# Row sums once a quarter behind a product with V, their pair sums accumulated on VectorE, and four conversions moved between VectorE, ScalarE and GpSimd

## The chip, the cores and the metric

One core of a Trainium2 chip runs the whole layer. The time is what one execution takes on the device, in microseconds (us). PE is TensorE (PEld its weight loads), DVE is VectorE, ACT is ScalarE, POOL is GpSimd, SP is SyncE, which here only issues DMAs.

## The reference

A transformer layer with causal attention (ALiBi bias) and a mixture of experts side by side on the same normed input. Batch 4, 1024 tokens, width 512, 16 heads of 32, 8 experts of inner size 352, two per token.

```
xn = layernorm(x)
q, k, v = (xn @ W.T + b) per head            # 4 x 16 heads x 1024 x 32
scores = q @ k.T / sqrt(32), causal, - slope_h * |i - j|
out = (softmax(scores) @ v) @ Wo.T + bo
combine = top 2 of softmax(xn @ gate_w.T), normalised
moe = sum_e combine_e * ((silu(g_e) * u_e) @ w2_e.T),   g_e, u_e = xn @ w1_e.T
return x + out + moe
```

Softmax is computed without its division: P = exp(scores - bound), O = P V, and the row sums R = P 1; O is divided by R at the end. The bias of v can be added before the product (each row of P/R sums to one) or after the division.

## The kernel before

Numbers that enter TensorE in the projections, the scores and the experts are split into two float16 halves, high and low, and multiplied in three passes. P and V stay float32.

Attention goes through 16 groups `G` (4 batches x 4 groups of four heads), each in 40 units `u` of one head: a unit's scores are 256 keys by 256 queries (three or four matmuls, L1266 to L1271), then one exp on ScalarE (L1864) from one of two PSUM halves `C` into `PT[t % 3]`. Four units, one for each head, make a tile `t`: tile `(q, i)` holds key pair `i` of query quarter `q`, with `i` from 0 to `q`. So a group has ten tiles; four of them (`i == q`) lie on the diagonal, and there only three of the four 128 x 128 blocks are computed (the exp is 384 wide, not 512). A quarter's product with V and its row sums gather in one of two PSUM banks, `O` and `M`, in columns 0 to 255 and 256 to 511.

For each tile GpSimd adds the two key blocks (`add`, L1984, 1024 elements a partition, 512 on the diagonal) into one of three buffers `PS`. TensorE multiplies the tile by V (`pv`, L1284) and, later, the sum by a block of ones (`rsum`, L1294; on the diagonal L1296 and L1297). Four heads go to four column strips of 32. The profile shows each of these float32 matmuls as two MATMUL instructions, so a group of 8 instructions is one row sum of four heads.

After a quarter's last row sum ScalarE copies the bank out (`osb`, L1895), a DMA folds the sums, VectorE inverts them (`rcp`, L1680), a DMA and a matmul (`bc`, L1306) spread them, VectorE scales (`a32`, L1684), and GpSimd splits the result into halves (`aT`: a cast, L1994, and a subtraction, L1995) for the output projection (L1318, evicted at L1691).

Beside this run, for the next groups: the projections of q and k (L1205; evicted by ScalarE at L1842 as `qk32`, rounded to the high half by VectorE at L1644 as `qkh`, low half on GpSimd at L1973 as `qkl`), V (L1222; evicted by VectorE at L1657 as `vsb`, bias added there), the row maxima that bound the scores (`pre` on TensorE, L1238 and L1243; `mx` on VectorE, L1671, and a small `join`, L1676), the layernorm of the next batch (its low half `xnl` on VectorE, L1556), the splitting of the expert weights (L1906 on ScalarE, L1725 on VectorE) and the routing (among it L1742). All but the tile sums and the two banks `C`, `O`/`M` share four PSUM banks `PB`: a bank is borrowed for a product and given back when its reader (VectorE, now and then ScalarE) is done.

The order is written out by a planner, `plan()`: it walks through the units, adds a unit's score and exp, fires events that were put at this unit (`at(u, f)`), and fills in projections by a credit of TensorE time. Every engine issues its own steps in this one order and never passes a step that waits. After the last unit come the output projection of the last batch and 71 slots of expert work, the stage from about 1155 us on.

## Time and profile before

| | |
|---|---|
| median of 3 runs | 1599.04 us (1596.22 to 1602.14) |
| profiled execution, its own time | 1600.13 us |
| its span, first to last instruction | 1598.3 us |
| mean granted TensorE clock | 0.966 of full |
| busy in the span: PE, DVE, POOL, ACT | 1465.1, 936.9, 848.4, 703.9 us |

1.8 us of the execution lie outside the span. Busy time is the union of an engine's instructions. The ends of matmuls are modelled and they overlap, so the distance from the start of one group of matmuls to the start of the next says more than a duration does. "Idle before" of a group of instructions is idle time of its engine just ahead of them, with what ended it; "issue" there means that no wait in the profile accounts for it.

### The profile page before, as it was taken

What the parts mean: (1) busy time and instruction counts of PE and PEld (TensorE: products, weight loads), DVE (VectorE), ACT (ScalarE), POOL (GpSimd) and SP (SyncE); (2) the same over time, 40 slices, a digit from 0 to 9 for tenths busy, and PEclk for the clock granted to TensorE, in tenths of its full rate; (3) what the DMA queues carried; (4) which work ended last, traced back from release to release, by engine and by line L of the source; (5) the groups of instructions that cost most, each with busy time, mean ns of one, the idle gap of its engine ahead of it and who ended that gap; (6) DMA issues with size and microseconds to landing.
All of it is one profiled execution on the core that took longest, in us unless ns stands there. A gap on an engine that the chain in (4) does not pass through costs nothing.

```text
span 1598.3 us, 35194 instructions
## 1 busy us (share of the span) xinstructions
PE 1465.1 (92%) x13499; PEld 862.9 (54%) x13499; DVE 936.9 (59%) x1765; ACT 703.9 (44%) x1179; POOL 848.4 (53%) x732
## 2 busy tenths in 40 slices
PE   4689989998998999999999899897789999999995
PEld 2356555654655565555565456553356565655663
DVE  7667877766687666668768976560143333333331
ACT  5245565545556555556664444465022222222221
POOL 5134555444454454545564446575117777668774
PEclk9899998999998999999999999998899999999998
DMA  7244433443524426343233310233867888889983
GB/s 252 57 130 135 140 94 108 119 132 105 161 81 116 136 85 209 92 126 102 89 107 112 100 41 16 68 126 101 303 161 131 133 129 137 125 120 148 147 138 44
DMA packets 189309, 193.92 MB, mean 121 GB/s; under 512 B 104900, under 2 KB 138948, under 8 KB 189021
## 3 DMA queue, kind: packets, MB, share of 16 engines
q1 hardware_dynamic: 160636, 152.27, 35.6%
q0 software_dynamic: 26128, 37.24, 14.0%
q8 instruction: 115, 1.88, 0.5%
q10 hardware_dynamic: 2384, 2.16, 0.4%
q14 instruction: 46, 0.37, 0.1%
HBM read 93.14 MB, written 53.74 MB: 92 GB/s over the span
## 4 chain that ended last, share of the span: by engine, by line
PE 67%; DVE 11%; DMA 8%; ACT 4%; issue 4%; POOL 3%; SPq 2%; ACTq 0%; another core or an unknown queue 0%; DVEq 0%; POOLq 0%
PE S L1356 13%; PE T L1205 4%; PE S L1205 4%; PE M L1284 4%; PE O L1387 4%; PE M L1387 4%; PE S L1238 3%; DVE arena L1671 3%; PE T L1238 3%; PE S L1266 3%; DMA arena<-arena 3%; PE O L1284 3%; DMA out<-arena 2%; PE T L1222 2%; PE T L1318 2%
## 5 line engine op out<-in xcount | busy, mean ns | idle before, releaser
L1864 ACT ACTIVATE arena<-S,psl 128x512 f32<-128x512 f32 (+1 forms) x640 | 401.8, 642 | 359.2 <-PE S L1268 194.4
L1984 POOL TENSOR_TENSOR arena<-arena 128x1024 f32<-128x1024 f32 (+1 forms) x160 | 312.3, 1954 | 215.9 <-ACT arena L1864 215.4
L2038 POOL DMA_INDIRECT out<-arena x142 | 222.1, 1564 | 110.2 <-issue 46.7
L1356 PE MATMUL S<-arena 128*128 x1704 | 267.4, 314 | 6.1 <-issue 4.9
L1671 DVE TENSOR_REDUCE arena<-S 128x1 f32<-128x512 f32 (+3 forms) x311 | 202.8, 656 | 103.5 <-PE S L1243 53.2
L1671 DVE TENSOR_REDUCE arena<-T 128x1 f32<-128x512 f32 (+3 forms) x297 | 193.7, 656 | 87.1 <-PE T L1243 49.1
L1356 PEld LDWEIGHTS S<-arena 128*128 128x128 f16 x1704 | 166.8, 98 | 103.7 <-issue 7.4
L1266 PE MATMUL S<-arena 106*128 106x256 f16 x640 | 179.3, 280 | 22.4 <-ACT arena L1864 21.2
L1973 POOL TENSOR_TENSOR arena<-arena 128x512 f16<-128x512 f32 x64 | 78.9, 1233 | 153.9 <-DVE arena L1644 153.7
L1783 DVE COPY arena<-T 128x512 f16<-128x512 f16 x71 | 30.2, 425 | 219.8 <-PE T L1371 181.9
L1238 PE MATMUL T<-arena 105*128 105x512 f16 (+3 forms) x382 | 113.1, 333 | 25.0 <-DMA arena<-in_up 10.1
L1917 ACT ACTIVATE arena<-S,sc 128x352 f32<-128x352 f32 x71 | 39.3, 553 | 206.4 <-PE S L1356 191.6
L1238 PE MATMUL S<-arena 105*128 105x512 f16 (+3 forms) x386 | 119.2, 341 | 9.7 <-DVE arena L1671 5.1
L1205 PE MATMUL T<-arena 128*128 128x512 f16 x420 | 108.3, 386 | 1.7 <-DVE arena L1671 0.7
L1266 PEld LDWEIGHTS S<-arena 106*128 106x128 f16 x640 | 63.6, 99 | 80.4 <-ACT arena L1864 38.7
L1994 POOL CAST arena<-arena 128x256 f16<-128x256 f32 x64 | 27.2, 425 | 150.2 <-DVE arena L1684 150.0
L1268 PE MATMUL S<-arena 106*128 106x256 f16 x384 | 106.7, 279 | 0.0
L1284 PE MATMUL M<-arena 128*32 128x256 f32 (+1 forms) x1536 | 99.3, 376 | 0.0
L2025 POOL DMA_INDIRECT arena<-xn_d,tl x71 | 72.6, 1023 | 43.9 <-DMA arena<-arena 22.3
L1205 PE MATMUL S<-arena 128*128 128x512 f16 x348 | 92.0, 388 | 1.9 <-DVE arena L1671 1.9
L1725 DVE SCALAR_TENSOR_TENSOR arena<-arena,sc 128x704 f16<-128x704 f32 (+2 forms) x56 | 70.0, 1250 | 34.5 <-ACT arena L1906 34.2
L1925 ACT ACTIVATE arena<-arena 128x352 f16<-128x352 f32 x71 | 35.2, 496 | 109.4 <-DVE arena L1769 101.7
(218 smaller groups left out, 2517.3 us busy)
## 6 DMA issues: line engine op xcount, KB each, us to landing
arena<-arena SPq DMA_DIRECT2D x192, 128.0 KB, 2.8
arena<-in_w1T SPq DMA_DIRECT2D x64, 352.0 KB, 3.6
arena<-in_x SPq DMA_DIRECT2D x64, 256.0 KB, 4.4
w_d<-arena SPq DMA_DIRECT2D x32, 352.0 KB, 2.8
arena<-w_d SPq DMA_DIRECT2D x16, 704.0 KB, 6.7
arena<-in_w2T SPq DMA_DIRECT2D x32, 256.0 KB, 3.0
out<-arena SPq DMA_DIRECT2D x32, 256.0 KB, 3.2
xn_d<-arena SPq DMA_DIRECT2D x24, 256.0 KB, 2.6
```

The source lines that it names most:

```text
L1205: tp = pe.matmul(z[:, :], wqkv[:, w_, c, f:f + P], xnT[:, a, c, half * 512:half * 512 + 512], start=(third == 0 and c == 0), stop=(third = ...
L1238: tp = pe.matmul(z[:, n * w:(n + 1) * w], stk[G % 2][0:KROWS - 1, h, 0, j * P:(j + 1) * P], stk[G % 2][0:KROWS - 1, h, 1, k0:k1], start=(n ...
L1266: pe.matmul(z[:, 0:2 * P], K[0], stk[G % 2][0:KROWS, h, 0, q0:q2], start=True, stop=False)
L1268: tp = pe.matmul(z[:, 2 * P:4 * P], K[1], stk[G % 2][0:KROWS, h, 0, q0:q2], start=False, stop=True)
L1284: tp = pe.matmul(YB[o.bank["pv", G, q]][D * x:D * x + D, f:f + n], V[(G + 1) % 3][:, 2 * i + k, x * D:(x + 1) * D], PT[t % 3][:, x, c:c + ...
L1356: tp = pe.matmul(y[:, i * 512:i * 512 + I], xT[:, s % XDEEP, 4 * a + c, :], weights[:, bass.ds(reg[s] + (w_ * NX * W1N + c * 2 * I + i * I ...
L1387: tp = pe.matmul(z[:, :], aTm[0:n, v, 2 * c + a, :], weights[0:n, bass.ds(r2 + (2 * NX * W1N + w_ * NX * W2N + c * E), E)], start=(k == 0) ...
L1671: dve.tensor_reduce(d[:, heads[0]:heads[-1] + 1], z, AX, ALU.max).then_inc(sems["mx"], 1)
L1864: act.activation(PT[t % 3][:, h, 0:n], CB[o.bank["score", u]][:, 0:n], ACT.Exp, scale=psl[:, hh:hh + 1]).then_inc(sems["exp"], 1)
L1973: pool.tensor_tensor(st[:, 2 * qk + 1, lo:hi], t32_at(*key), st[:, 2 * qk, lo:hi], ALU.subtract).then_inc(sems["qkl"], 1)
L1984: pool.tensor_tensor(PS[t % 3][:, :, f:f + n], PT[t % 3][:, :, f:f + n], PT[t % 3][:, :, c:c + n], ALU.add).then_inc(sems["add"], 1)
L2038: pool.indirect_dma_start(out=halves, out_offset=bass.IndirectOffsetOnAxis(row[:, part, s:s + 1].bitcast(U32), 0), in_=yo[:, s % YDEEP, c0 ...
```

## The change

Row sums. For a quarter's first tile GpSimd adds the two key blocks into an accumulator `AC[q % 2]` (for quarter 0 a copy and an add of 512). For a later tile it adds them into a buffer, `PSF` (whole tiles) or `PSD` (diagonal), one of each, and a new VectorE step `acc` adds this buffer to the accumulator; on the diagonal GpSimd itself adds the first block, so its one add becomes two of 512. TensorE multiplies the accumulator by ones once a quarter, in the step that comes behind the next tile's product with V. The exp no longer waits for a row sum.

Conversions. `qkh` and `vsb` go from VectorE to ScalarE; `vsb` becomes a plain scaled copy, and the bias of v is added in a new ScalarE step `aTh` (two ACTIVATEs of 128 x 256), which also makes the high half that GpSimd's cast made. The low half `xnl` goes from VectorE to GpSimd for the later batches. One load (`bvb`) at the start goes. Some distances in the plan are a unit or two longer.

```diff
             at(u + 1, lambda: add("add", t))
+            if i:
+                at(u + 4, lambda: add("acc", t))
             at(4 * t + 5, lambda: products(t))
-            at(4 * t + (10 if i < q else 9), lambda: sums(t))
+            if t == QUADS - 1:
+                at(4 * t + 9, lambda: sums(t))
...
         add("pv", t)
+        if i == 0 and t:
+            sums(t - 1)
...
-        if i == q:
-            at(now[0] + 1, lambda: emptied(G, q))
+        at(now[0] + 1, lambda: emptied(G, q))
...
-                add("aT", G, q)
-                ready["aT", G, q] = now[0] + 2
+                at(now[0] + 1, lambda: add("aTh", G, q))
+                at(now[0] + 2, lambda: add("aT", G, q))
+                ready["aT", G, q] = now[0] + 4
...
                 on.wait_ge(*at("add", t))
+                if i:
+                    on.wait_ge(*at("acc", t))
                 for x in range(4):
-                    R = YB[o.bank["pv", G, q]][D * x:D * x + D, 2 * P:4 * P]
-                    if i < q:
-                        tp = pe.matmul(R, ones, PS[t % 3][:, x, :], start=False, stop=False)
-                    else:
-                        pe.matmul(R[:, 0:P], ones, PT[t % 3][:, x, 0:P], start=False, stop=False)
-                        tp = pe.matmul(R[:, P:2 * P], ones, PS[t % 3][:, x, P:2 * P], start=False, stop=True)
+                    tp = pe.matmul(YB[o.bank["pv", G, q]][D * x:D * x + D, 2 * P:4 * P], ones, AC[q % 2][:, x, :],
+                                   start=False, stop=True)
...
+            elif kind == "acc":
+                t, = key
+                G, q, i = quad(t)
+                on.wait_ge(*at("add", t))
+                f, z = (0, PSF) if i < q else (P, PSD)
+                if i > 1:
+                    on.wait_ge(*at("acc", t - 1))
+                dve.tensor_tensor(AC[q % 2][:, :, f:], AC[q % 2][:, :, f:], z, ALU.add).then_inc(sems["acc"], 1)
...
+                act.activation(st[:, 2 * qk, lo:hi], t32_at(*key), ACT.Copy).then_inc(sems["qkh"], 1)
...
+                act.activation(V[(G + 1) % 3][:, 4 * half:4 * half + 4, :].rearrange("p a n -> p (a n)"),
+                               PB[o.bank["v", b, g, half]][:, :], ACT.Copy, scale=col(CV)).then_inc(sems["vsb"], 1)
...
+                a_ = osb[:, q % 2, 0:2 * P]
+                act.activation(aT[:, 0, g, 2 * q * P:2 * (q + 1) * P], a_, ACT.Identity, bias=bvs[:, g:g + 1])
+                act.activation(a_, a_, ACT.Identity, bias=bvs[:, g:g + 1]).then_inc(sems["aTh"], 1)
...
+                elif i < q:
+                    if t > 10:
+                        on.wait_ge(*at("acc", t - 1 if i == 2 else t - 3 if q == 3 else t - 6))
+                    elif i == 2 or q == 3:
+                        on.wait_ge(*at("acc", t - 1 if i == 2 else t - 3))
+                    pool.tensor_tensor(PSF, y[:, :, 0:2 * P], y[:, :, 2 * P:4 * P], ALU.add).then_inc(sems["add"], 1)
+                else:
+                    if G or q > 1:
+                        on.wait_ge(*at("acc", t - (3, 3, 4)[q - 1]))
+                    pool.tensor_tensor(PSD, y[:, :, P:2 * P], y[:, :, 2 * P:3 * P], ALU.add)
+                    if i > 1:
+                        on.wait_ge(*at("acc", t - 1))
+                    else:
+                        on.wait_ge(*at("add", t - 1))
+                    pool.tensor_tensor(z[:, :, 0:P], z[:, :, 0:P], y[:, :, 0:P], ALU.add).then_inc(sems["add"], 1)
```

How this moves instructions is shown at three places. First TensorE, around unit 466, where a whole tile's row sum stood by itself between two units. Before (L1266 and L1268 are scores, L1294 the row sum, L1238 a piece of the maxima, L1222 the projection of V, L1306 `bc`, L1253 a transposition of maxima):

```order
L1266 MATMUL S<-arena 128x256 [waits s_exp]
L1268 MATMUL S<-arena 128x256
L1294 MATMUL O<-arena,cF 32x256 [waits s_add]
L1294 MATMUL O<-arena,cF 32x256 x3
L1238 MATMUL T<-arena 128x512 [waits s_mx]
L1222 MATMUL S<-arena 128x128 x12
L1266 MATMUL S<-arena 128x256 [waits s_exp]
L1268 MATMUL S<-arena 128x256
L1306 MATMUL T<-arena 128x256 [waits s_unfold1,s_mx]
L1253 MATMUL S<-cF,arena 4x128 [waits s_mx]
L1253 MATMUL S<-cF,arena 4x128
```

The same units now (lines are those of the new file: L1271 and L1273 scores, L1243 the maxima, L1227 V, L1309 `bc`, L1258 the transposition):

```order
L1271 MATMUL S<-arena 128x256 [waits s_exp]
L1273 MATMUL S<-arena 128x256
L1243 MATMUL T<-arena 128x512 [waits s_mx]
L1227 MATMUL S<-arena 128x128 x12
L1271 MATMUL S<-arena 128x256 [waits s_exp]
L1273 MATMUL S<-arena 128x256
L1309 MATMUL T<-arena 128x256 [waits s_unfold1,s_mx]
L1258 MATMUL S<-cF,arena 4x128 [waits s_mx]
L1258 MATMUL S<-cF,arena 4x128
```

The row sum is gone from there, and with it a change between the two shapes of matmul. The quarter's one row sum (L1299) stands three units later, at the end of the quarter, behind the next quarter's first product (L1289):

```order
L1271 MATMUL S<-arena 128x256 [waits s_exp]
L1273 MATMUL S<-arena 128x256
L1289 MATMUL M<-arena 32x256 [waits s_osb]
L1289 MATMUL M<-arena 32x256 x7
L1299 MATMUL O<-arena,cF 32x256 [waits s_acc,s_add]
L1299 MATMUL O<-arena,cF 32x256 x3
L1243 MATMUL S<-arena 128x512 [waits s_mcp]
L1227 MATMUL S<-arena 128x128 x12
```

It follows the product at once and waits for VectorE's `acc` as well as for GpSimd's `add`. Second VectorE, from one `a32` to the next around the middle of attention. Before (L1684 `a32`, L1671 maxima, L1644 `qkh`, L1725 a weight's low half, L1680 `rcp`):

```order
L1684 TENSOR_TENSOR arena<-arena,T 128x256 [waits s_bc]
L1671 TENSOR_REDUCE arena<-S 128x1 [waits s_pre]
L1671 TENSOR_REDUCE arena<-T 128x1 [waits s_pre]
L1680 RECIPROCAL arena<-arena 128x8 [waits s_fold1]
L1671 TENSOR_REDUCE arena<-S 128x1 [waits s_pre] x2
L1644 CAST arena<-arena 128x512 [waits s_qk32]
L1725 SCALAR_TENSOR_TENSOR arena<-arena,sc 128x704 [waits s_wsh]
L1671 TENSOR_REDUCE arena<-S 128x1 [waits s_pre]
L1671 TENSOR_REDUCE arena<-T 128x1 [waits s_pre,s_mtr]
L1671 TENSOR_REDUCE arena<-S 128x1 [waits s_pre] x2
L1657 SCALAR_TENSOR_TENSOR arena<-T,sc,arena 128x512 [waits s_pv,s_v]
L1684 TENSOR_TENSOR arena<-arena,T 128x256 [waits s_bc]
```

Now, up to the same `a32` (L1664; L1643 maxima, L1660 `rcp`, L1656 `acc`, L1705 a weight's low half):

```order
L1643 TENSOR_REDUCE arena<-S 128x1 [waits s_pre]
L1643 TENSOR_REDUCE arena<-T 128x1 [waits s_pre]
L1643 TENSOR_REDUCE arena<-S 128x1 [waits s_pre]
L1660 RECIPROCAL arena<-arena 128x8 [waits s_fold1]
L1643 TENSOR_REDUCE arena<-S 128x1 [waits s_pre]
L1656 TENSOR_TENSOR arena<-arena 128x1024 [waits s_add]
L1643 TENSOR_REDUCE arena<-S 128x1 [waits s_pre]
L1705 SCALAR_TENSOR_TENSOR arena<-arena,sc 128x704 [waits s_wsh]
L1643 TENSOR_REDUCE arena<-T 128x1 [waits s_pre,s_mtr]
L1643 TENSOR_REDUCE arena<-S 128x1 [waits s_pre] x2
L1656 TENSOR_TENSOR arena<-arena 128x4x128 [waits s_acc,s_add]
L1664 TENSOR_TENSOR arena<-arena,T 128x256 [waits s_bc]
```

`qkh` and `vsb` (L1657) have left the queue, and two `acc`, which wait for GpSimd's `add`, stand ahead of maxima that free banks for TensorE. Third ScalarE, in the second group. Before (L1864 exp, L1871 a row of maxima, L1842 `qk32`):

```order
L1871 ACTIVATE arena<-S 4x256 [waits s_mrow2,s_mtr]
L1842 ACTIVATE arena<-T,bq,cq 128x512 [waits s_qk,s_qkl]
L1864 ACTIVATE arena<-S,psl 128x384 [waits s_score,s_add,s_pv]
L1864 ACTIVATE arena<-S,psl 128x384 [waits s_score] x3
L1864 ACTIVATE arena<-S,psl 128x512 [waits s_score,s_add,s_pv]
```

Now (L1875 exp, L1882 a row of maxima, L1822 `qk32`, L1855 and L1856 `aTh`, L1832 `qkh`):

```order
L1882 ACTIVATE arena<-S 4x256 [waits s_mrow2,s_mtr]
L1822 ACTIVATE arena<-T,bq,cq 128x512 [waits s_qk,s_qkl]
L1875 ACTIVATE arena<-S,psl 128x384 [waits s_score,s_add,s_pv]
L1875 ACTIVATE arena<-S,psl 128x384 [waits s_score]
L1855 ACTIVATE arena<-arena,bvs 128x256 [waits s_a32]
L1856 ACTIVATE arena<-arena,bvs 128x256
L1832 ACTIVATE arena<-arena 128x512 [waits s_stack12,s_stack11,s_stack13,s_stack10,s_qk32]
L1875 ACTIVATE arena<-S,psl 128x384 [waits s_score] x2
```

Between two exps stand three instructions more, and two of the waits are for VectorE and for DMAs (`stack`).

## Rows read from the trace of the kernel before

**Rows 1.** Busy us (instructions) by stretch: PE, PEld, DVE, ACT, POOL; then clock, DMA share, GB/s.
```profile
130.00:1080.00 950.00, 899.67 (x9472) 531.19 (x9465) 678.51 (x1218) 512.82 (x854) 487.95 (x441) 0.97 0.38 109
200.00:800.00 600.00, 567.12 (x5977) 330.92 (x5973) 417.72 (x691) 338.87 (x561) 297.69 (x289) 0.96 0.40 117
800.00:960.00 160.00, 152.88 (x1552) 90.19 (x1552) 130.66 (x310) 79.59 (x134) 79.91 (x63) 0.99 0.32 90
```

**Rows 2.** What PE waited for, 130 to 1080 us: in total, times, longest.
```profile
PE S L1266 <- ACT arena L1864: 10.8, 12, 2.3
PE T L1238 <- DVE arena L1671: 4.1, 7, 1.2
...
PE S L1253 <- DVE arena L1671: 0.4, 1, 0.4
```

**Rows 3.** PE in order of time: start, length, instructions merged.
```profile
646.97 0.64 PE L1294 MATMUL O<-arena,cF 128*32 128x256 f32 x8
647.54 0.39 PE L1238 MATMUL S<-arena 105*128 105x512 f16 x1
...
657.68 0.45 PE L1296 MATMUL O<-arena,cF 128*32 128x128 f32 x8
657.92 0.42 PE L1297 MATMUL O<-arena,cF 128*32 128x128 f32 x8
658.14 1.07 PE L1284 MATMUL M<-arena 128*32 128x256 f32 x16
659.14 0.39 PE L1238 MATMUL S<-arena 105*128 105x512 f16 x1
```

**Rows 4.** Row sums of whole tiles, by line: count, busy us, mean ns, idle before.
```profile
L1294 PE MATMUL M<-arena,cF 128*32 128x256 f32 x512 | 42.2, 402 | 2.5 <-POOL arena L1984 2.5
L1294 PE MATMUL O<-arena,cF 128*32 128x256 f32 x256 | 20.9, 399 | 0.0
```

**Rows 5.** VectorE's groups that leave, or are nearest to what comes.
```profile
L1644 DVE CAST arena<-arena 128x512 f16<-128x512 f32 x64 | 40.1, 627 | 10.9 <-ACT arena L1842 5.9 <-DMA arena<-arena 4.8
L1657 DVE SCALAR_TENSOR_TENSOR arena<-S,sc,arena 128x512 f32<-128x512 f32 x17 | 12.7, 746 | 1.4 <-PE S L1222 1.2
L1556 DVE TENSOR_TENSOR arena<-arena 128x512 f16<-128x512 f32 x24 | 17.9, 746 | 2.9 <-ACT arena L1798 2.1
L1742 DVE TENSOR_TENSOR arena<-cF,posf 128x1024 f32<-128x1024 f32 x8 | 12.7, 1589 | 0.0
L1676 DVE TENSOR_TENSOR arena<-arena 128x8 f32<-128x8 f32 x32 | 18.6, 581 | 1.1
```

**Rows 6.** Shortest, median and longest ns, first and last start: two VectorE lines, GpSimd's `add`.
```profile
L1742 DVE TENSOR_TENSOR arena<-cF,posf x8: 1215/1549/2114, 940.7 to 1019.5; 128x1024 f32<-128x1024 f32 x8
L1676 DVE TENSOR_TENSOR arena<-arena x32: 166/168/2346, 78.9 to 1082.0; 128x8 f32<-128x8 f32 x32
L1984 POOL TENSOR_TENSOR arena<-arena x160: 1257/2354/3021, 87.3 to 1120.2; 128x1024 f32<-128x1024 f32 x96, 128x512 f32<-128x512 f32 x64
```

**Rows 7.** GpSimd and VectorE in order of time around one small add.
```profile
469.63 4.67 POOL L1984 TENSOR_TENSOR arena<-arena 128x1024 f32<-128x1024 f32 x2
469.67 2.35 DVE L1676 TENSOR_TENSOR arena<-arena 128x8 f32<-128x8 f32 x1
```

**Rows 8.** ScalarE's groups, for the price of what is moved there.
```profile
L1864 ACT ACTIVATE arena<-S,psl 128x512 f32<-128x512 f32 x384 | 258.4, 686 | 205.0 <-PE S L1268 194.4 <-DVE arena L1680 3.0 <-remote 2.9
L1864 ACT ACTIVATE arena<-S,psl 128x384 f32<-128x384 f32 x256 | 146.0, 577 | 154.2 <-PE S L1271 150.7 <-PE O L1284 1.4 <-ACT arena L1895 0.7
L1798 ACT ACTIVATE arena<-arena 128x512 f16<-128x512 f32 x32 | 19.6, 627 | 38.1 <-DVE arena L1550 38.1
L1933 ACT ACTIVATE arena<-O,tl 128x512 f32<-128x512 f32 x36 | 24.2, 672 | 6.7 <-PE O L1387 6.7
```

**Rows 9.** GpSimd's groups.
```profile
L1994 POOL CAST arena<-arena 128x256 f16<-128x256 f32 x64 | 27.2, 425 | 150.2 <-DVE arena L1684 150.0
L1964 POOL TENSOR_TENSOR arena<-arena 128x512 f16<-128x512 f32 x8 | 9.5, 1210 | 3.3 <-ACT arena L1798 3.3
```

109 lines of the change are left out of this document (51 added, 58 removed).

## The prediction, written before the changed kernel was run

> **What bounds the kernel.** I read four views, in this order. The busy times by stretch [rows 1]: while attention runs with its fill (130 to 1080 us) TensorE is busy 899.7 of 950 us, VectorE 678.5, ScalarE 512.8, GpSimd 488.0. Then what TensorE waited for in that stretch [rows 2]: 10.8 us for exps, and 23.0 us in fourteen rows (4.1 to 0.4 us each, the first and the last are shown) for VectorE to give back a bank, with a few single waits beside them. A wait for GpSimd's `add` hardly exists (2.5 us over the whole run [rows 4]). So TensorE sets the pace from 130 to 1080 us, and time taken from it comes off the end as long as nobody else falls behind. The reader should see there that VectorE is second, with 71% on average and 82% between 800 and 960 us (130.7 of 160 [rows 1]), where the routing runs. The expert stage after about 1155 us is touched nowhere by the change; I price it at nothing.
>
> **TensorE: what leaves.** A matmul's length says little, since they overlap; I go by starts. The row sum of a whole tile is 8 instructions; there are 768 of them, 96 groups, busy 42.2 + 20.9 = 63.1 us, 0.66 us a group [rows 4]. All are removed. A diagonal row sum is 16 instructions of half the width and stands directly ahead of the next product: from its start at 657.68 to the product's at 658.14 are 0.46 us [rows 3]. Four a group of heads, 64 in all: 29.4 us.
>
> **TensorE: what comes.** 64 row sums of 8 instructions, each behind a product of the same shape (256 columns, 32-wide strips). A product of 16 such instructions takes 1.00 us from its start to the next start (658.14 to 659.14), a lone row sum of 8 takes 0.57 (646.97 to 647.54) [rows 3]. Both end with the same change to another shape of matmul, so 8 more instructions in one run cost the difference, 0.43 us. Below it lies what 8 half-wide ones take (657.68 to 657.92, 0.24 [rows 3]), above it a lone group's 0.66. 64 x 0.43 = 27.5 us (15 to 42). TensorE's balance: 63.1 + 29.4 - 27.5 = 65.0 us less (50 to 77).
>
> **VectorE.** It loses 64 roundings of q and k (40.1 us), 32 copies of V (12.7 us for 17, 23.9 for all by the same 0.746), and 24 low halves (17.9) [rows 5]: 81.9 us. It gains 96 `acc`: six a group of heads, half with 1024 elements, half with 512. Nothing in the trace is this instruction. The nearest with 1024 float32 elements and two operands in SBUF is L1742: 1.215 us at best, 1.589 in the mean; an add of 8 elements, L1676, takes 0.166 at best [rows 5, 6], and half-way between them lies 0.69 for 512. These, 1.215 and 0.69, are the lower ends. The upper ends come from what such adds suffer here: the one of 8 elements takes 0.168 us in the median and 2.346 at worst [rows 6], and that worst one began 0.04 us after the first of two GpSimd adds and ended when that one did (4.67 us for two [rows 7]). So a whole GpSimd add, 2.34 us, may come on top: 3.56 and 3.03 us. The mean of the small add is 0.581, which is 0.41 above its median [rows 5, 6]; I take 1.59 and 0.69 + 0.41 = 1.10. 48 x 1.59 + 48 x 1.10 = 129 us (91 to 316). Net VectorE has 47 us more to do (9 to 234).
>
> The Trainium skill bears on this: "SBUF — State Buffer", section "Who interferes with whom", says that a VectorE instruction with two SBUF inputs contends with a GpSimd instruction that reads SBUF, and that whichever starts first keeps the shared ports for its whole length. The trace agrees with that in the 2.35 us of the small add. By that rule the delay also goes the other way, and `acc` holds up GpSimd's adds; this is the third rival below, whose numbers are from rows 6 and 7.
>
> Does it fit? A group of heads takes 65 us now (160 tiles, ten a group, whose adds start from 87.3 to 1120.2 [rows 6], so 6.5 us a tile) and gains 65.0 / 16 = 4.1 us; VectorE gets 129 / 16 = 8.1 and loses 4.0 (without `xnl`). From 200 to 800 us (9.2 groups): 417.7 + 38 - 18 = 438 of 562 us, 78% instead of 70%. From 800 to 960 us (2.5 groups): 130.7 + 10.1 = 141 of 150 us, 94% instead of 82%. In that last stretch I give back half of the 10 us gained: 5 us. Elsewhere the 23 us that TensorE waits for VectorE's banks grow: idle room on VectorE shrinks from 29 to some 20%, and I let the waits grow by half: 12 us (0 to 40). `acc` waits for GpSimd's `add`, and the maxima that free the banks are queued behind it. It is issued three units after the `add`, 4.6 us, against the add's 2.34 us (2.5 for the diagonal's two, by 1.257 each [rows 6]), so mostly it finds its operand ready. The row sum on TensorE waits for `acc`, issued two units (3.1 us) ahead; with 1.1 to 1.6 us for it a late VectorE shows here first, and scores are queued behind: 2 us.
>
> **ScalarE.** 64 `qkh`, SBUF to SBUF with 512 elements, at 0.627 (L1798): 40.1 us. 32 `vsb` at 0.672 (a scaled PSUM copy, L1933): 21.5. 128 halves of `aTh` with 256 elements: the exp shows 0.686 for 512 and 0.577 for 384, so 0.468 for 256: 59.9 [rows 8]. Together 121 us, no bounds needed beyond a tenth either way. In 130 to 1080 us that makes about 627 of 911 us, 69% instead of 54%. An exp may start later by up to two of these (1.3 us) and TensorE has two score halves, so two units of 1.5 us cover it, except where an exp was already late (10.8 us of waits [rows 2]); I add 6 us (0 to 20). `aTh` waits for VectorE's `a32` with exps queued behind it, so a late VectorE reaches the scores here too. In the 6 us are also the two waits of 4.8 us in all for the stack DMAs [rows 5], which now stop exps instead of maxima.
>
> **GpSimd.** 48 adds of 512 more at 1.257 [rows 6] (60 us), 16 copies at about twice the cast's 0.425 (14), 24 `xnl` at 1.21 (29), less 64 casts (27) [rows 9]: 76 us more, about 558 of 911 us in the stretch, 61%. Its new waits are for `acc` of an earlier tile, since there is one buffer, with `qkl` and `aT` queued behind; by the order that `acc` is issued a unit before. Its own queue does not get long; what it costs others is in the terms above.
>
> **The ends.** At the start the first four roundings take ScalarE 0.627 each as they take VectorE in the mean, but stand in a queue with its other conversions: 0.8 us, an estimate of one more of them ahead. In the tail the last quarter's chain has two ScalarE instructions of 0.47 in place of a cast of 0.42: 0.5 us.
>
> **The sum.** 65.0 gained; 5 + 12 + 2 + 6 + 1.3 = 26 given back; 39 us less. Against the profiled execution's own 1600.1 us (span 1598.3 and 1.8 around it): 1561 us. The median of the runs, 1599.0, is 1.1 lower, too close to matter; I say 1560.
>
> **Rivals.**
> First, it all converts: `acc` and the ScalarE steps fall into idle time. For it: no engine but TensorE is over 82% in any stretch. Against: queues are strict, and VectorE and TensorE already wait for each other in both directions. 1600 - 65 + 1.3 gives 1536 us.
> Second, VectorE becomes the bound in good part: it is the second engine, it gets 47 us net, and the banks hang on it. Price: the waits for banks grow by 36 us instead of 12, and all 10 us between 800 and 960 us are lost. 1561 + 24 + 5 gives about 1588 us.
> Third, slower than before: the accumulations and GpSimd's adds block each other. `acc` for tile t comes about when GpSimd begins the add of tile t + 1, if VectorE lags by a unit. Each of 96 then waits up to 2.34 us [rows 6, 7] with maxima behind it, a bank is kept, and TensorE stops. It decides from 65 / 96 = 0.68 us of TensorE standing still per `acc`. At 1.0 us each it is 96 us against 65, and 1600 + 31 gives 1631 us. Against it: the mean wait of the small adds is 0.41 us, well under 0.68, and four banks give slack.
> Fourth, no change: TensorE is not the bound although it looks busy. PEld is busy only 531 of 950 us [rows 1], and a chain through exps and banks could set the pace, with the row sums in its gaps. Against it: TensorE's named waits are some 40 us, so there are no gaps for 92 us of row sums. 1598 us. The Trainium skill takes that side: "Perfetto Trace Analysis", section "Identifying the Most-Contended Engine", calls matmul occupancy a bad measure of the distance to the roofline and asks for the weight loads' share, here 56%. By the waits of this trace the queue is full all the same.
>
> **Chances.** My forecast (1548 to 1578) 0.50; all converts 0.18; VectorE bound 0.20; no change 0.05; slower 0.07. The second and third of these cover 1530 to 1548 and 1578 to 1592. The range from 1536 to 1592 leaves out the last two cases (0.12) and a little below and above, 0.2 in all, and it takes in the bounds of the row sum's price and of the waits. A measurement here can tell 0.5%, 8 us, from no change: faster 0.87, within 0.5% 0.05, slower 0.08.
>
> **What would show it.** Right: TensorE's busy time falls by about 65 us and all of the loss of span lies ahead of 1120 us; row sums are 512 instructions of some 27 us; `acc` has a mean near 1.3 us with a longest one over 3; VectorE is 90% busy or more in the routing stretch; TensorE's waits for VectorE's banks and for exps come to 50 us or so. If `acc` lies at its lower ends and the bank waits stay at 23 us, the first rival holds. If TensorE shows long waits for `acc` at the row sum, or if it falls to the lower clock in attention for long, my sum is wrong: neither is in it but for 2 us.

## The result

The changed kernel takes 1601.0 us in the median of 20 runs (1595.9 to 1607.1), against 1594.4 us for the kernel before on the same chip (20 runs); the ratio is 1.0041 with an interval of [1.0022, 1.0059]. So it is no faster, and slower by a trifle, below the 0.5% at which the prediction drew its line. The prediction was 1560 us, with 1536 to 1592 as its range. It was wrong.

### The profile page after: what moved, and what is told of

Read it like the earlier page. It is cut to its first block, busy times and chain, and to the rows that moved or that the text cites. A ratio compares the mean times of both kernels' runs of the same rounds, so it can differ in the third digit from the quotient of the medians.

```text
span 1595.9 us, 32893 instructions
## 1 busy us (share of the span) xinstructions
PE 1419.4 (89%) x12219; PEld 838.9 (53%) x12219; DVE 947.9 (59%) x1742; ACT 799.1 (50%) x1403; POOL 948.4 (59%) x756
## 4 chain that ended last, share of the span: by engine, by line
PE 55%; DVE 13%; POOL 11%; DMA 7%; issue 6%; ACT 4%; SPq 4%; ACTq 0%; POOLq 0%; DVEq 0%
PE S L1359 15%; PE O L1390 4%; PE M L1390 4%; DVE arena L1643 4%; PE T L1210 3%; DVE arena L1656 3%; DMA arena<-arena 3%; PE M L1289 3%; PE S L1210 3%; PE S L1243 2%; SPq L1059 2%; PE T L1243 2%; PE S L1271 2%; PE O L1289 2%; POOL arena L2006 2%
## 5 line engine op out<-in xcount | busy, mean ns | idle before, releaser
L1875 ACT ACTIVATE arena<-S,psl 128x512 f32<-128x512 f32 (+1 forms) x640 | 399.5, 641 | 256.0 <-PE S L1273 152.2
L1643 DVE TENSOR_REDUCE arena<-S 128x1 f32<-128x512 f32 (+3 forms) x311 | 202.0, 655 | 113.5 <-PE S L1248 82.4
L1643 DVE TENSOR_REDUCE arena<-T 128x1 f32<-128x512 f32 (+3 forms) x297 | 193.0, 654 | 95.5 <-PE T L1248 65.3
L1271 PE MATMUL S<-arena 106*128 106x256 f16 x640 | 182.0, 285 | 40.7 <-ACT arena L1875 39.2
L1999 POOL TENSOR_TENSOR arena<-arena 128x512 f32<-128x512 f32 (+1 forms) x64 | 135.7, 2121 | 81.5 <-ACT arena L1875 81.4
L1984 POOL TENSOR_TENSOR arena<-arena 128x512 f16<-128x512 f32 x64 | 79.9, 1250 | 165.2 <-ACT arena L1832 165.0
L2006 POOL TENSOR_TENSOR arena<-arena 128x1024 f32<-128x1024 f32 x48 | 114.8, 2392 | 75.4 <-ACT arena L1875 46.9
L1243 PE MATMUL S<-arena 105*128 105x512 f16 (+3 forms) x386 | 120.3, 345 | 21.8 <-DVE arena L1643 12.7
L1243 PE MATMUL T<-arena 105*128 105x512 f16 (+3 forms) x382 | 115.8, 342 | 26.4 <-DMA arena<-in_up 10.4
L1656 DVE TENSOR_TENSOR arena<-arena 128x512 f32<-128x512 f32 (+1 forms) x96 | 110.3, 1148 | 36.0 <-POOL arena L2015 19.4
L1271 PEld LDWEIGHTS S<-arena 106*128 106x128 f16 x640 | 64.4, 101 | 103.1 <-ACT arena L1875 61.4
L1273 PE MATMUL S<-arena 106*128 106x256 f16 x384 | 107.3, 280 | 0.0
L2051 POOL DMA_INDIRECT arena<-xn_d,tl x71 | 73.1, 1030 | 46.3 <-DMA arena<-arena 25.8
L1289 PE MATMUL M<-arena 128*32 128x256 f32 (+1 forms) x1536 | 100.3, 380 | 0.0
L2010 POOL TENSOR_TENSOR arena<-arena 128x512 f32<-128x512 f32 x48 | 67.9, 1415 | 41.6 <-ACT arena L1875 41.5
```

The costliest lines, as they stand in the source:

```text
L1243: tp = pe.matmul(z[:, n * w:(n + 1) * w], stk[G % 2][0:KROWS - 1, h, 0, j * P:(j + 1) * P], stk[G % 2][0:KROWS - 1, h, 1, k0:k1], start=(n ...
L1271: pe.matmul(z[:, 0:2 * P], K[0], stk[G % 2][0:KROWS, h, 0, q0:q2], start=True, stop=False)
L1289: tp = pe.matmul(YB[o.bank["pv", G, q]][D * x:D * x + D, f:f + n], V[(G + 1) % 3][:, 2 * i + k, x * D:(x + 1) * D], PT[t % 3][:, x, c:c + ...
L1643: dve.tensor_reduce(d[:, heads[0]:heads[-1] + 1], z, AX, ALU.max).then_inc(sems["mx"], 1)
L1656: dve.tensor_tensor(AC[q % 2][:, :, f:], AC[q % 2][:, :, f:], z, ALU.add).then_inc(sems["acc"], 1)
L1875: act.activation(PT[t % 3][:, h, 0:n], CB[o.bank["score", u]][:, 0:n], ACT.Exp, scale=psl[:, hh:hh + 1]).then_inc(sems["exp"], 1)
```

## The profile after

Two of the stretches of [rows 1] again, of the changed kernel, with the same columns:

```profile
130.00:1080.00 950.00, 855.09 (x8255) 506.95 (x8254) 684.24 (x1194) 591.33 (x1046) 581.49 (x464) 0.95 0.37 108
800.00:960.00 160.00, 146.23 (x1374) 86.82 (x1375) 133.87 (x311) 92.67 (x166) 95.23 (x65) 0.98 0.33 92
```

TensorE is busy 44.6 us less in the same 950 us, and the work gets no further in them: that is idle time. Over the whole execution its busy time fell from 1465.1 to 1419.4 us, by 45.7 and not by 65, and the span from 1598.3 to 1595.9 us. The difference between 65 and 45.7 is the clock, as far as an estimate can tell. In the two profiled executions it stood at 0.966 in the mean before and stands at 0.952 now; with full speed (2.4 GHz) or half (1.2 GHz) as its two levels that is (1 - 0.966) x 2 x 1598 = 109 us at half speed before, and 153 us after. In 44 more such microseconds work that needs 22 at full speed is done, so 22 us are added to busy time: 65 - 22 = 43, and 45.7 is seen. (The kernel below with only the conversions moved has the same matmuls as the kernel before and checks this: 109 us at half speed before and 78 there should make 15 us less of busy time, and 1465.1 - 1449.0 = 16.1 us is seen.) Of the 45.7 us that left busy time only 2.4 left the span; the other 43.3 us became idle time.

What TensorE waited for from 130 to 1080 us in the changed kernel, columns as in [rows 2]:

```profile
PE S L1271 <- ACT arena L1875: 29.0, 22, 4.3
PE S L1243 <- DVE arena L1643: 10.9, 9, 2.9
PE M L1299 <- DVE arena L1656: 7.9, 4, 3.9
PE T L1243 <- DVE arena L1643: 7.1, 5, 3.5
PE S L1258 <- DVE arena L1643: 5.1, 1, 5.1
PE S L1243 <- DVE arena L1664: 4.6, 5, 1.9
...
PE O L1299 <- DVE arena L1656: 1.1, 1, 1.1
```

Scores waiting for exps (L1271 for L1875) are 29.0 us where they were 10.8 [rows 2]; row sums waiting for `acc` (L1299 for L1656) are 9.0 us, which is new. All rows in which TensorE waits for VectorE add up to 44.4 us against the 23.0 of [rows 2]: 29.4 for maxima (L1643; 20.0 before), 6.0 for `a32` (L1664; 3.0 before) and these 9.0 for `acc`.

One part of why exps are late stands in ScalarE's own waits in the same stretch:

```profile
ACT arena L1906 <- POOL arena L2021: 14.1, 5, 4.3
ACT arena L1855 <- DVE arena L1664: 8.0, 6, 3.7
ACT arena L1832 <- DMA arena<-arena: 7.9, 4, 5.2
```

L1906 is `osb`, the copy of a quarter's output to SBUF. It may not overwrite its buffer until GpSimd's `aT` (L2021) has read it, and exps are queued behind it. The other two are `aTh` behind `a32`, and `qkh` behind the stack's DMAs (7.9 us; the maxima waited 4.8 for them before [rows 5]).

The groups of instructions that the change made, columns as in [rows 4]:

```profile
L1656 DVE TENSOR_TENSOR arena<-arena 128x1024 f32<-128x1024 f32 x48 | 68.8, 1434 | 16.6 <-POOL arena L2006 16.1
L1656 DVE TENSOR_TENSOR arena<-arena 128x512 f32<-128x512 f32 x48 | 41.4, 863 | 19.4 <-POOL arena L2015 19.4
L1299 PE MATMUL M<-arena,cF 128*32 128x256 f32 x256 | 21.5, 409 | 7.9 <-DVE arena L1656 7.9
L1299 PE MATMUL O<-arena,cF 128*32 128x256 f32 x256 | 21.2, 403 | 1.1 <-DVE arena L1656 1.1
L1832 ACT ACTIVATE arena<-arena 128x512 f16<-128x512 f32 x64 | 40.0, 626 | 8.0 <-DMA arena<-arena 7.9
L1855 ACT ACTIVATE arena<-arena,bvs 128x256 f16<-128x256 f32 x64 | 32.0, 501 | 29.5 <-DVE arena L1664 29.4
L2006 POOL TENSOR_TENSOR arena<-arena 128x1024 f32<-128x1024 f32 x48 | 114.8, 2392 | 75.4 <-ACT arena L1875 46.9 <-DVE arena L1656 28.2
L2015 POOL TENSOR_TENSOR arena<-arena 128x512 f32<-128x512 f32 x48 | 67.0, 1397 | 7.0 <-DVE arena L1656 7.0
```

`acc` took 110.2 us (68.8 + 41.4), under the 129 predicted. Ahead of it VectorE stood idle 35.5 us for GpSimd's adds, and GpSimd stood idle 35.2 us for `acc` (the last two rows). Each engine waits for the other.

One such meeting, all engines in order of time (start, length, instruction; idle time before it and what ended it in brackets):

```profile
1036.98 0.42 PE L1271 MATMUL S<-arena 106*128 106x256 f16 x1
1037.19 0.42 PE L1273 MATMUL S<-arena 106*128 106x256 f16 x1
...
1038.44 0.27 PE L1271 MATMUL S<-arena 106*128 106x256 f16 x1
1038.56 0.27 PE L1273 MATMUL S<-arena 106*128 106x256 f16 x1
...
1039.20 1.07 PE L1289 MATMUL O<-arena 128*32 128x256 f32 x16
1039.42 1.28 POOL L2015 TENSOR_TENSOR arena<-arena 128x512 f32<-128x512 f32 x1
1040.65 2.35 POOL L1999 TENSOR_TENSOR arena<-arena 128x1024 f32<-128x1024 f32 x1
1040.74 2.81 DVE L1656 TENSOR_TENSOR arena<-arena 128x512 f32<-128x512 f32 x1 [2.82 <-POOL arena L2015]
1043.47 0.41 DVE L1664 TENSOR_TENSOR arena<-arena,T 128x256 f32<-128x256 f32 x1
1043.69 0.64 PE L1299 MATMUL M<-arena,cF 128*32 128x256 f32 x8 [3.42 <-DVE arena L1656]
...
1043.91 0.51 ACT L1855 ACTIVATE arena<-arena,bvs 128x256 f16<-128x256 f32 x1 [3.70 <-DVE arena L1664]
```

GpSimd ends a diagonal's second add at about 1040.7 and begins its next add, 2.35 us long, at once. VectorE, which had waited 2.82 us for the first, starts `acc` 0.09 us behind the second and is through 0.55 us after it ended: 2.81 us for 512 elements, of which the shortest took 0.64. TensorE stood 3.42 us at the row sum, with every score queued behind, and ScalarE 3.70 us at `aTh`. The first two pairs show the clock: from one matmul's start to the next are 0.21 us at 1037 and 0.12 at 1038.5, the same instruction at half and at full clock (granted 0.52 of full from 1036.5 to 1038.0 and 1.00 from 1038.4 to 1039.2).

The second meeting has the wait of `osb` in it, which the kernel before never showed, again in order of time:

```profile
496.21 0.19 POOL L1966 TENSOR_TENSOR nw<-nw 128x4 f32<-128x4 f32 x1
...
499.91 0.22 POOL L1970 TENSOR_SCALAR nw<-nw 128x4 f32<-128x4 f32 x1
500.21 1.15 POOL L1984 TENSOR_TENSOR arena<-arena 128x512 f16<-128x512 f32 x1
...
501.33 2.33 POOL L1999 TENSOR_TENSOR arena<-arena 128x1024 f32<-128x1024 f32 x1
501.34 2.61 DVE L1553 TENSOR_SCALAR arena<-arena,mv,nw 128x512 f32<-128x512 f32 x1
503.63 0.84 POOL L2021 TENSOR_TENSOR arena<-arena 128x256 f16<-128x256 f32 x1
...
504.47 0.53 DVE L1553 TENSOR_SCALAR arena<-arena,mv,nw 128x512 f32<-128x512 f32 x1
504.50 0.60 ACT L1906 ACTIVATE arena<-M 128x512 f32<-128x512 f32 x1 [4.27 <-POOL arena L2021]
505.00 0.68 ACT L1875 ACTIVATE arena<-S,psl 128x512 f32<-128x512 f32 x1
505.73 0.40 PE L1271 MATMUL S<-arena 106*128 106x256 f16 x1 [4.35 <-ACT arena L1875]
```

Ahead of `aT` GpSimd's queue has thirteen small instructions of the next batch's layernorm (L1966 to L1970, from 496.21 to 500.13), then `qkl` (L1984) and one pair sum (L1999); ScalarE waits 4.27 us at `osb`, and TensorE 4.35 us for the exp behind it. Three of the five waits of `osb`, 12.7 of the 14.1 us, stand behind this same sequence, once in each batch that has a next one. The kernel before has the same small instructions and never waits there, since its cast and subtraction stand ahead of the next pair sum; the changed plan puts `aT` two units later, behind `aTh`. With only the conversions moved the three waits are 2.2 us each; with row sums accumulated the diagonal's second add stands ahead of the small instructions, and they are 4.2. Beside GpSimd's add even VectorE's scaling of x (L1553) takes 2.61 us; the next one, alone, 0.53.

## The experiments

All ratios are against the kernel before, from the same chip, with their 95% intervals; microseconds between two kernels are the difference of their ratios times 1595. A difference of two is uncertain by some 5 to 8 us. The first kernel is the one before with one edit, as are two later ones; the others start from the changed kernel. Where a kernel leaves out part of the row sums, its result is wrong and only its time is used; that is said with it. The stretch from 130 to 1080 us is a fixed piece of time: in a kernel that is faster it holds some of what comes behind attention, so waits and idle time are compared between kernels over the whole execution, in the table behind the experiments.

### Row sums behind the next product, nothing else

```
-            at(4 * t + (10 if i < q else 9), lambda: sums(t))
+            if t == QUADS - 1:
+                at(4 * t + 9, lambda: sums(t))
...
         add("pv", t)
+        if t:
+            sums(t - 1)
```

> The kernel before with each tile's row sum put directly behind the next tile's product with V; the work is the same, only 96 changes of matmul shape go. If TensorE is the bound: 96 x (0.66 - 0.43) = 22 us less, about 1573 us. If it is not: within 8 us of before.

Measured: 1588.6 us, 0.9955 [0.9936, 0.9974], 7 us less. A place behind a product is worth that, with every row sum kept, and not the 22 us of the first theory: TensorE's busy time fell from 1465.1 to 1449.3 us, and its idle time grew by 8.5 us.

### The conversions moved, the row sums as before

The changed kernel without `acc`, with row sums, pair sums and their buffers as before (the later places of `aTh` and `aT` and the other distances of the new plan stay):

```
-            if i:
-                at(u + 4, lambda: add("acc", t))
-            if t == QUADS - 1:
-                at(4 * t + 9, lambda: sums(t))
+            at(4 * t + (10 if i < q else 9), lambda: sums(t))
```

> The changed kernel with the row sums as before (no accumulation on VectorE, three pair-sum buffers, a row sum for every tile), so the moved conversions alone. Theory 1 (the accumulation ate the gain): no slower than before, 1590 to 1600 us, or a little faster, since VectorE has 82 us less to do. Theory 2 (ScalarE and GpSimd became late with the moved work): 20 to 50 us slower than before.

Measured: 1575.8 us, 0.9888 [0.9861, 0.9914], 18 us less. Its stretch of 130 to 1080 us:

```profile
130.00:1080.00 950.00, 904.95 (x9658) 534.01 (x9656) 595.72 (x1121) 613.84 (x1081) 506.35 (x419) 0.98 0.38 111
```

TensorE is busier than before (904.95 against 899.67 us) at a better clock, with VectorE 83 us lighter and ScalarE 101 us heavier. Over the whole execution its waits for VectorE fall from 27.0 to 14.8 us and its scores' waits for exps stay at 21.2 us, although `osb` waits 7.8 us for `aT` here already:

```profile
ACT arena L1897 <- POOL arena L1993: 7.8, 6, 2.2
```

The part of the change that the prediction booked mostly as a cost is its gain.

### Without accumulations

```
-            if i:
-                at(u + 4, lambda: add("acc", t))
...
-                if i:
-                    on.wait_ge(*at("acc", t))
```

> The changed kernel without the VectorE accumulation: pair sums are still formed on GpSimd, in the same number of instructions, but those of later whole tiles are dropped, and a row sum waits for GpSimd alone. Theory 1: the 65 us appear, 1535 to 1550 us. Theory 2: only the accumulation's own small waits go, 1585 to 1600 us.

Measured: 1554.4 us, 0.9763 [0.9733, 0.9794]. GpSimd's waits for `acc` are gone too, and on the diagonal it writes its sum straight into the accumulator; the row sums lack what `acc` would have added. `acc` and its waits cost the difference to the changed kernel, 0.0278 or 44 us.

### Accumulations of two elements a head, all waits kept

```
-                dve.tensor_tensor(AC[q % 2][:, :, f:], AC[q % 2][:, :, f:], z, ALU.add)
+                dve.tensor_tensor(z[:, :, 0:2], z[:, :, 0:2], PSF[:, :, 0:2], ALU.add)
```

> The changed kernel with the accumulation on VectorE cut to 2 of 256 (or 128) elements a head: every instruction and every wait of it stays, its length goes (most of the row sum is left out; on the diagonal GpSimd writes its sum instead of VectorE adding it). Theory A (the waits between GpSimd, VectorE and TensorE cost the time): it stays near the changed kernel, 1590 to 1600 us. Theory B (the time on VectorE and at the shared ports costs it): it falls to the kernel without accumulation, 1554 to 1565 us.

Measured: 1567.2 us, 0.9826 [0.9794, 0.9859]. Here too GpSimd writes the diagonal's sum straight into the accumulator. The waits, with instructions of some 0.3 us each (28.0 us in all), cost 10 us over the kernel without `acc`.

### Accumulations that read one input

A maximum over the same elements into four numbers stands in place of each addition:

```
+                z = PSF if i < q else AC[q % 2][:, :, P:]
+                dve.tensor_reduce(scr[:, :], z, AX, ALU.max).then_inc(sems["acc"], 1)
```

> As the kernel with the tiny accumulation, but each accumulation is a maximum over the same 1024 or 512 elements of one buffer: about as long on VectorE as the real one, with one operand in SBUF instead of two (its result is thrown away). If the length on VectorE costs the time (B1): 1585 to 1600 us. If the contention of two-operand adds with GpSimd costs it (B2): near 1555 to 1570 us, and GpSimd's adds come down from 2.39 us toward their 2.34.

Measured: 1586.2 us, 0.9938 [0.9913, 0.9962]. Its substitutes, by shortest, median and longest in nanoseconds, and below them the real `acc` of the changed kernel:

```profile
L1657 DVE TENSOR_REDUCE scr<-arena x96: 645/944/1221, 106.8 to 1115.6; 128x4 f32<-128x512 f32 x48, 128x4 f32<-128x1024 f32 x48
```

```profile
L1656 DVE TENSOR_TENSOR arena<-arena x96: 642/1210/2836, 105.0 to 1126.4; 128x512 f32<-128x512 f32 x48, 128x1024 f32<-128x1024 f32 x48
```

As in the two kernels before this one, row sums are incomplete. With one input none is ever stretched (1.221 at most); with two, the same bulk takes up to 2.836 us. The length alone costs 18 us over the tiny ones, and the step to the real `acc` another 16 us, though the 96 instructions got only 110.2 - 90.6 = 19.6 us longer. That step is called the second input below, but it also brings an output of full width in place of four numbers; no run has the two apart.

### The accumulation on GpSimd instead

```
-                    pool.tensor_tensor(PSF, y[:, :, 0:2 * P], y[:, :, 2 * P:4 * P], ALU.add)
+                    then(pool.tensor_tensor(z, z, y[:, :, 0:2 * P], ALU.add))
+                    pool.tensor_tensor(z, z, y[:, :, 2 * P:4 * P], ALU.add)
```

> The changed kernel with the accumulation on GpSimd instead of VectorE: two adds of 1024 for a later whole tile, three of 512 on the diagonal. GpSimd gets 48 x 2.39 = 115 us more, VectorE 110 us less. If VectorE's queue was what took the gain and GpSimd has room (581 + 115 of 950 us): 1560 to 1575 us. If GpSimd's adds now hold up the exps through the three tile buffers: 1600 us or more.

Measured: 1628.5 us, 1.0202 [1.0169, 1.0234]. The stretch:

```profile
130.00:1080.00 950.00, 834.76 (x8101) 500.22 (x8103) 619.14 (x1088) 578.84 (x1022) 695.25 (x535) 0.95 0.36 103
```

GpSimd is busy 73% of it, no engine is full, and it is the slowest kernel of all: another 26 us over the changed one. Its trace shows one large new wait of TensorE in the same stretch:

```profile
PE T L1163 <- POOL arena L1963: 22.6, 8, 8.7
PE S L1163 <- POOL arena L1963: 14.9, 4, 8.0
```

L1163 are the transpositions of the next batch's x, and L1963 is `xnl`, which the change moved to GpSimd and which now stands behind two or three adds a tile. These waits are 37.5 us; in the changed kernel they are 4.0.

### Conversions moved and row sums behind the products

> The conversions moved, row sums for every tile as before but each directly behind the next product with V. By the two alone (0.9888 and 0.9955 of before) 0.984, about 1570 us; if the freed VectorE lets TensorE use what the 96 saved changes of shape give (22 us), 1560 us.

The first two edits together. Measured: 1567.6 us, 0.9841 [0.9803, 0.9878]. With all the work in it, this is the fastest version that computes the reference: 25 us under the kernel before, at a clock of 0.976. What the two gained apart, 18 and 7 us, adds up.

### 48 row sums fewer in the kernel before

This and the next ask what the prediction took for granted: does time taken from TensorE come off the end?

```
-            at(4 * t + (10 if i < q else 9), lambda: sums(t))
+            if i in (0, q):
+                at(4 * t + (10 if i < q else 9), lambda: sums(t))
```

> The kernel before, with the row sums of the 48 whole tiles that are neither a quarter's first nor its diagonal left out (384 of the 768 matmul instructions of that line; the sums come out too small). TensorE has 48 x 0.66 = 31.5 us less work and no other engine has an instruction more or less. What the prediction took for granted, that TensorE sets the pace of attention: 1594 - 31 = 1563 us, ratio 0.980. The rival, that the chain of scores, maxima and exps sets it and the row sums stand in its gaps: 1585 to 1594 us, ratio 0.994 to 1.000, with the idle time of TensorE between 130 and 1080 us up by about what its busy time lost.

(With all 96 left out the results are no longer finite, and there is no time for it.) Measured: 1577.2 us, 0.9869 [0.9839, 0.9900]: 21 us of 31.5, between both expectations. The stretch, and the score's wait in it:

```profile
130.00:1080.00 950.00, 888.54 (x9214) 532.88 (x9210) 679.38 (x1226) 518.76 (x869) 495.01 (x448) 0.96 0.38 110
```

```profile
PE S L1267 <- ACT arena L1865: 21.2, 20, 2.3
```

No other engine's work was touched. It is tempting to set the 21.2 us against the 10.8 of [rows 2], and the idle time of 61.5 us against 50.3; but attention ends 18 us earlier here, so this stretch holds 18 us of later work more, and the kernel before has ten of its microseconds of waits for exps behind 1080 us. Over the whole executions the scores' waits for exps are

```profile
PE S L1266 <- ACT arena L1864: 21.2, 21, 2.5
PE S L1267 <- ACT arena L1865: 25.8, 25, 2.3
```

and TensorE's idle time grows by 3.2 us only, from 133.2 to 136.4. The larger part of the missing third is in the clock: 0.958 against 0.966 in the two profiles makes 133 us at half speed against 109, so 12 us of the 31.5 come back as slower work. Over all runs the mean granted clock is 0.962 against 0.967, which makes 8 us of it.

### The same 48 fewer, with the conversions moved

> The kernel with the conversions moved alone, with the same 48 row sums left out; again only TensorE loses work, 31.5 us of it. The conversions alone took 1576 us (0.989) at a granted clock of 0.975. If TensorE sets the pace there: 1576 - 31 = 1545 us, ratio 0.969. If freed time on TensorE turns into idle time and half clock: 1565 to 1576 us, ratio 0.982 to 0.989, with a granted clock under 0.975. The kernel changed without accumulations left out 54 of 65 us of row sums and stood at 0.976, so I expect something near 0.978.

Measured: 1554.3 us, 0.9731 [0.9708, 0.9755], 25 us of 31.5 over the conversions alone. That more of it converts with VectorE lighter (25 us against 21) is within what these differences are uncertain by, so it is not shown.

### Low halves of x alone, and all conversions but them

```
-            elif kind == "xnl" and key[0]:
...
-                dve.tensor_tensor(XH[k][:, E:2 * E], x_place(b, half, i), XH[k][:, 0:E],
-                                  ALU.subtract).then_inc(sems["xnl"], 1)
...
-            elif kind == "xnl" and not key[0]:
+            elif kind == "xnl":
```

> The kernel before with one conversion moved: the 24 low halves of x that VectorE made (17.9 us) are made by GpSimd. In the kernel before TensorE stood idle 7.7 us in the 24 transposes around them, with the conversions moved not at all. Theory: this is most of the gain of the conversions, 0.5 us a transpose and the scores behind it: 1582 to 1586 us, ratio 0.992 to 0.995. Rival: the gain comes from VectorE being freed of q, k and V (64 us of the 82), and this alone gives 1590 to 1594 us, ratio 0.998 to 1.000.

Measured: 1592.2 us, 0.9982 [0.9964, 1.0000], 3 us. The second kernel is the conversions without this edit.

> The conversions moved alone, but with the 24 low halves of x kept on VectorE as in the kernel before. Theory that the low halves made the gain: 1584 to 1590 us, ratio 0.994 to 0.997. Rival, that freeing VectorE of q, k and V made it: 1576 to 1581 us, ratio 0.989 to 0.992.

Measured: 1586.9 us, 0.9944 [0.9922, 0.9966], 9 us. My theory that the low halves made the gain falls by the first and is held up by the second: 3 and 9 do not make 18. Either the parts help each other (the scarcer VectorE's work, the more each piece counts), or the intervals of 3 us each way hide a sum. That stays open.

### No accumulations and no second add on GpSimd

The kernel without accumulations, and in it:

```
                    pool.tensor_tensor(z[:, :, P:2 * P], y[:, :, P:2 * P], y[:, :, 2 * P:3 * P], ALU.add)
-                    pool.tensor_tensor(z[:, :, 0:P], z[:, :, 0:P], y[:, :, 0:P], ALU.add)
```

> The kernel changed without accumulations (1554 us, ratio 0.9763, granted clock 0.961), and in it also without GpSimd's second add on the 48 diagonals behind a quarter's first tile, so that the row sums lack those terms as well; the reciprocals are replaced by copies of the same 8 elements, since a sum can be zero then. GpSimd loses 48 instructions of some 1.4 us, 68 us, TensorE, ScalarE and VectorE nothing. Its row sums on TensorE took 36 us against the 64 of the kernel with the conversions moved and 48 row sums fewer, which stands at 0.9731 all the same. Theory: GpSimd's extra adds hold up the exps' buffers and cost what those 28 us should have given: 1530 to 1537 us, ratio 0.960 to 0.965. Rival, that the exps on ScalarE now set the pace of the scores whatever is taken off TensorE: 1550 to 1556 us, ratio 0.973 to 0.977, with the idle time ahead of the scores for exps (25.5 us in 24 waits) as before.

Reciprocals are copies here, of the same size. Measured: 1543.7 us, 0.9678 [0.9653, 0.9703], between the two expectations. The 48 adds cost 14 us. How long `osb` waits for `aT` in the kernel without accumulations, and in this one:

```profile
ACT arena L1902 <- POOL arena L2009: 14.5, 6, 4.7
```

```profile
ACT arena L1902 <- POOL arena L2009: 9.9, 7, 2.6
```

And the scores' wait for exps, first without accumulations, then here:

```profile
PE S L1269 <- ACT arena L1871: 27.9, 27, 4.8
```

```profile
PE S L1269 <- ACT arena L1871: 27.4, 27, 3.3
```

The longest stalls are shorter (2.6 for 4.7 us, 3.3 for 4.8); the many short ones stay, so both theories hold a part.

### The sum from the runs

Conversions -18; 65 us less on TensorE, with nothing that delays it but 16 copies on GpSimd, -33 (0.9888 to 0.9678); the second add +14; the waits of `acc` +10; its length +18; its second input +16. Together +7 us. That this is the ratio of 1.0041 proves nothing, since each step starts where the one before it ends; in another order the single steps could come out otherwise.

What each step did to TensorE, over the whole profiled execution of each kernel. Idle is span less busy time; half speed is (1 - clock) x 2 x span; the last two columns add up the rows of `--waits`, the first all rows in which TensorE waits for VectorE, the second the scores' row for exps:

| kernel | ratio | busy | idle | at half speed | waits for VectorE | scores for exps |
|---|---|---|---|---|---|---|
| before | 1 | 1465.1 | 133.2 | 109 | 27.0 | 21.2 |
| before, 48 row sums fewer | 0.9869 | 1443.9 | 136.4 | 133 | 30.7 | 25.8 |
| conversions | 0.9888 | 1449.0 | 118.8 | 78 | 14.8 | 21.2 |
| conversions, behind products | 0.9841 | 1431.9 | 133.9 | 75 | 16.4 | 23.3 |
| no `acc`, no second add | 0.9678 | 1399.4 | 142.5 | 105 | 17.4 | 28.5 |
| no `acc` | 0.9763 | 1402.6 | 148.3 | 121 | 20.6 | 28.9 |
| `acc` of two elements | 0.9826 | 1411.8 | 158.8 | 129 | 32.4 | 33.3 |
| `acc` with one input | 0.9938 | 1415.7 | 171.9 | 133 | 41.9 | 36.3 |
| changed | 1.0041 | 1419.4 | 176.5 | 153 | 49.5 | 39.2 |

From the kernel without `acc` to the changed one idle time grows by 28.2 us and time at half speed by 32, which is 16 us of work: 44 us, as the ratios have it. The waits for VectorE grow by 28.9 us over the same rows, and those for exps by 10.3. So `acc` costs what it costs through VectorE's queue above all, and through the clock.

## Why the prediction was wrong, step by step

The prediction had 39 us less, the runs have 7 more. By the sum above, 25 of the 46 us between them lie in `acc`: its terms were 5 (routing stretch), 12 (banks) and 2 (row sum), 19 us, and it cost 44. Another 14 lie in GpSimd's second add, which had no term. The rest of the change (65 less 6 for ScalarE and 1.3 at the ends, 58 us) gave 51, near its price, but by luck: 65 us less on TensorE gave 33, and the conversions, which had no gain of their own in the sum, gave 18.

**"TensorE sets the pace, and time taken from it comes off the end."** This step failed in its size. The two kernels with 48 row sums fewer show 21 and 25 us for 31.5, and the full 65 us gave 33. The proviso, "as long as nobody else falls behind", was read from busy shares. What came between is a lower clock and waits: from the conversions alone to the kernel without `acc` and second add, idle time grows from 118.8 to 142.5 us and time at half speed from 78 to 105. The fourth rival, a chain through exps and banks, got 0.05. By its own number, 1598 us, it came nearest, but not by its mechanism: on TensorE's side half of the time did convert. The Trainium skill, "Perfetto Trace Analysis", section "Identifying the Most-Contended Engine", says that the matmul busy share does not measure well how close a kernel is to the roofline. No run here measures that distance; a TensorE 95% busy gave back two thirds of what was taken from it.

**TensorE's balance of 65.0 us.** It holds. Busy time with half of the time at half speed taken off is 1465.1 - 54.3 = 1410.8 us before and 1419.4 - 76.6 = 1342.8 after, 68 us less. The row sum behind a product adds what was said; of the changed kernel, in order of time:

```profile
497.46 1.07 PE L1289 MATMUL O<-arena 128*32 128x256 f32 x16
498.35 0.61 PE L1299 MATMUL M<-arena,cF 128*32 128x256 f32 x8
498.89 0.34 PE L1243 MATMUL S<-arena 105*128 105x384 f16 x1
```

From the product's start to the score's are 1.43 us, and 1.00 without the row sum [rows 3]: 0.43 us, the price taken. (The sign "512 instructions of some 27 us" sets this price by starts against busy time: the trace has 42.7 us busy, 21.5 + 21.2.) What the sum did not have is the clock: 44 us more at half speed, some 20 us of work time. The prediction named this as a way to be wrong and gave it no number.

**Banks, 12 us.** In the stretch the waits for maxima grew from 20.0 to 29.4 us and those for `a32` from 3.0 to 6.0: 12.4 in all, as priced, but by luck. The conversions alone bring VectorE's waits down to 9.5 us there, and the kernel without `acc` has 15.5; with `acc` they are 44.4, of which 35.4 are for banks.

**The row sum's wait for `acc`, 2 us.** It is 9.0, in five waits of up to 3.9 us.

**`acc` at 129 us.** 110.2 us, within the bounds and 15% under the forecast; the use of it was wrong. This is the step that failed most. The sum let these instructions fall into idle room on VectorE and charged for banks and one row sum; on the chip they cost 44 us on the end, 10 by their waits, 18 by their length and 16 by the second input. This is the mechanism of the third rival at about half its price: 0.46 us per `acc` (44 / 96), under the 0.68 from which it would have decided by itself. The rule that the prediction cited on shared ports held in kind: an `acc` of 2.81 us against 0.64. GpSimd's adds of 1024 beside it did not grow (2.392 us in the mean, and 2.391 in the kernel before, which has no `acc`), and those of 512 by 0.1 us (1.397 and 1.415 against 1.297), so here nearly all of the delay fell on VectorE.

**ScalarE, 6 us, and GpSimd, nothing.** The lengths were right to 7% (0.626 for 0.627, 0.501 for 0.468). ScalarE's term was not what failed: with only the conversions moved the scores wait as long for exps as before (21.2 us over the whole execution). In the changed kernel they wait 39.2. "Its own queue does not get long" is the step that failed, and with it the second add that was booked at nothing and cost 14 us. Where the layernorm's small instructions, `qkl` and a pair sum meet in GpSimd's queue, `aT` comes late, `osb` on ScalarE waits for it (0 before, 7.8 us with the conversions, 14.1 in the changed kernel), and exps stand behind `osb`. Without `acc` it is 14.5 us, and 9.9 without the second adds as well. The prediction looked at what is queued behind GpSimd's new waits and not at who, two engines on, has to wait for the last of them. How much of the 14 us comes by this way is not shown: with and without the second adds the scores' waits for exps are 28.9 and 28.5 us, while idle time differs by 5.8 us and time at half speed by 16.

**Conversions as a cost.** Taking 82 us from VectorE was only set against `acc`. Alone the conversions are worth 18 us, so the change consisted of a gain of that size and of a new way to sum rows that lost all of it. Which conversion makes the gain stays open; in the trace it shows as shorter waits for VectorE (27.0 to 14.8 us) and as 30 us less at half speed.

**800 to 960 us, 5 us.** VectorE reaches 84%, not 94%, and TensorE is 6.7 us less busy there. No run tests this stretch by itself.

**Two slips.** The second rival's own terms, 1561 + 24 + 5, give 1590 and not 1588 us. TensorE's named waits in the stretch add up to 49 us, not to some 40. Neither moves the forecast.

## What to carry to other kernels

When the fullest engine is fed by a chain that returns to it (here score, exp, bank, score), take some of its work out in one cheap run before pricing a rebuild: the yield was 67 and 79% at 31.5 us, and 51% at 65. Price each new instruction by the waits of those behind it in every queue it links, and not by the idle share of its engine; the waits of `acc` cost 10 us before it did any work, and GpSimd's second adds, on an engine busy 61%, cost 14. Compare traces of kernels of different length over the whole execution or from mark to mark: a fixed stretch made 5 us more of waits look like 10. Test a bundle's parts apart: the half that looked like overhead was the gain.
